# A slot's products with values stand between the two halves of the next slot's scores, in the normed and the causal attention of a decoder kernel

## The reference, cut to what matters

```
# L1 attention ("normed"): layernorm of q, k and v per head first
scores = jnp.einsum('bqhd,bkhd->bhqk', q, k) * scale
probs = jax.nn.softmax(scores, axis=-1)
out = jnp.einsum('bhqk,bkhd->bqhd', probs, v)
return out.reshape(b, s, NH * HD) @ Wo + bo

# L3 cross attention ("causal"): 77 context tokens stand ahead of x in keys and values
dots = jnp.einsum('bhid,bhjd->bhij', q, k) * scale
mask = j_idx > i_idx + mem_len
dots = jnp.where(mask[None, None], -jnp.inf, dots)
attn = jax.nn.softmax(dots, axis=-1)
```

## Time and profile before

| what | us |
|---|---|
| median of 3 runs | 9875.43 (9867.83 to 9891.36) |
| the profiled execution, its own time | 9900.52 |
| its span | 9898.7 |
| the normed stage's slots | about 2393 to 3492 |
| the causal stage's slots | about 7916 to 8768 |

### The profile page before, as it was taken

One profiled execution on the slowest core, in us unless ns is written; L12 is line 12 of the kernel. 1 busy time (PEld: TensorE's weight loads), 2 busy tenths in 40 slices (PEclk: granted clock), 3 DMA queues, 4 the chain that ended last, 5 costly groups with the idle time before them and its releaser, 6 DMA issues. The chain is left out here.

```text
span 9898.7 us, 124977 instructions
## 1 busy us (share of the span) xinstructions
PE 8326.5 (84%) x45542; PEld 4752.5 (48%) x45542; DVE 5787.9 (58%) x10909; ACT 4316.1 (44%) x7440; POOL 2034.5 (21%) x1786
## 2 busy tenths in 40 slices
PE   4888487985889979998998789888978699989998
PEld 1222255652333336645654344444434344458888
DVE  6778442025777736625643777874644365657776
ACT  3667231112555546514531556764312044444443
POOL 1110110211011001101100224432000011127776
PEclk8889666986999989999998889888977699989999
DMA  3222232212122100000000000000000133236665
GB/s 70 43 43 44 43 65 79 77 56 44 25 44 43 25 23 1 4 0 21 1 4 4 11 1 1 1 1 11 0 6 1 26 58 53 45 125 196 197 192 175
DMA packets 221123, 459.78 MB, mean 46 GB/s; under 512 B 51536, under 2 KB 87097, under 8 KB 219255
## 3 DMA queue, kind: packets, MB, share of 16 engines
q1 hardware_dynamic: 152935, 236.72, 11.9%
q0 software_dynamic: 67584, 215.02, 7.5%
HBM read 366.63 MB, written 71.33 MB: 44 GB/s over the span
## 5 line engine op out<-in xcount | busy, mean ns | idle before, releaser
L823 ACT ACTIVATE probs<-scores 128x1024 f32<-128x1024 f32 (+4 forms) x960 | 868.3, 937 | 885.0 <-PE scores L700 625.6
L912 DVE TENSOR_REDUCE row_max<-ring 128x1 f32<-128x512 f32 (+3 forms) x1792 | 1025.4, 626 | 239.3 <-PE ring L674 213.1
L700 PE MATMUL scores<-query_stack,key_stack 99*128 99x512 bf16 (+3 forms) x2816 | 853.9, 390 | 183.9 <-DVE levels L934 94.7
L3965 POOL DMA_INDIRECT r_got<-in_L_ffn_tables,r_index x768 | 784.7, 1022 | 453.9 <-DVE r_index L4261 202.5
L720 PE MATMUL outputs<-probs,head_values 128*32 128x512 f32 (+3 forms) x5632 | 764.9, 617 | 17.5 <-ACT probs L820 15.4
L820 ACT ACTIVATE probs<-levels,quant 128x1024 f32<-128x1024 uint8 x512 | 607.5, 1233 | 257.8 <-DVE levels L934 245.1
L674 PE MATMUL ring<-key_stack,query_stack 96*128 96x512 bf16 (+3 forms) x1792 | 608.7, 382 | 63.0 <-DMA key_stack<-normed_parts 39.6
L934 DVE TENSOR_SCALAR levels<-scores 128x1024 uint8<-128x1024 f32 x512 | 600.1, 1218 | 100.1 <-PE scores L700 96.7
L700 PEld LDWEIGHTS scores<-query_stack,key_stack 99*128 99x128 bf16 x2816 | 251.9, 103 | 714.9 <-DVE levels L934 310.1
L3783 DVE TENSOR_TENSOR_SCAN ssm_pre<-ssm_pre,added 128x1024 f32<-128x1024 f32 x256 | 571.0, 2271 | 31.2 <-ACT ssm_pre L3741 31.2
L3718 PE MATMUL state_sums<-term,constants 128*128 128x512 f32 x1024 | 497.9, 610 | 43.3 <-POOL term L3749 34.3
(11 more groups left out here) (695 smaller groups left out, 16237.8 us busy)
## 6 DMA issues: line engine op xcount, KB each, us to landing
joined_heads<-heads_out SPq DMA_DIRECT2D x512, 32.0 KB, 2.0
expert_w<-in_L_ffn_w SPq DMA_DIRECT2D x16, 1024.0 KB, 7.3
quant_parts<-parts SPq DMA_DIRECT2D x48, 256.0 KB, 5.5
query_stack<-quant_parts SPq DMA_DIRECT2D x48, 256.0 KB, 8.6
key_stack<-quant_parts SPq DMA_DIRECT2D x48, 256.0 KB, 8.4
query_stack<-cross_parts SPq DMA_DIRECT2D x48, 256.0 KB, 8.5
normed_parts<-parts SPq DMA_DIRECT2D x48, 256.0 KB, 5.2
query_stack<-normed_parts SPq DMA_DIRECT2D x48, 256.0 KB, 8.4
```

What stands on the lines that cost most here:

```text
L700: last = nc.tensor.matmul(out[:, off:GROUP], keys, q_stack[0:rows, h, half * GROUP + off:(half + 1) * GROUP], start=True, stop=not edge)
L823: nc.scalar.activation(dst, s_ps[0:k_rows, 2 * (e % 2):2 * (e % 2) + 2, off:GROUP], ACT.Exp, scale=scale).then_inc(probs_ready, 1)
L912: nc.vector.reduce_max(row_max[:, i, qt, at:at + 1], src[:, 0:cols], AX.X).then_inc(ring_read, 1)
L3965: nc.gpsimd.indirect_dma_start(out=got[:, k % GOT_ROWS, :], out_offset=None, in_=io["L3_ffn_tables"], in_offset=bass.IndirectOffsetOnAxis( ...
```

## The change

One line of `own_order` moves up by two: the products with values of slot n - 1 now stand behind place A of slot n and ahead of the second half of its scores.

```
             order += [("scores", n, 0)] if live else []
             order += [("values", n - 2)] if late and 0 <= n - 2 < len(slots) else []
             order += plan.get(3 * n, [])
+            order += [("values", n - 1)] if not late and 0 < n <= len(slots) else []
             order += [("scores", n, 1)] if live else []
             order += plan.get(3 * n + 1, [])
-            order += [("values", n - 1)] if not late and 0 < n <= len(slots) else []
             order += plan.get(3 * n + 2, [])
```

## The result

The changed kernel took 10041.86 us in the median of four runs (10035.65 to 10050.27), the kernel before 9875.85 (9867.83 to 9891.36, four runs): ratio 1.0167, 95% interval 1.0151 to 1.0183. That is +166 us where I had forecast +83, outside my range. The profiled execution took 10036.22 us (span 10034.1) against 9900.52 (span 9898.7), which is +136. The traces can only explain what is in them.

What follows compares the result with a forecast made beforehand. VectorE's reads through the three-bank ring bound mid-group slots, TensorE the projections, TensorE in step with ScalarE the tails. 48.3 + 4.7 + 9.1 + 21 = 83 us on 9875.4 gave 9958; 8-in-10 range 9905 to 10018.

Steps and rivals of the forecast that it cites:

- the ring's rule: Ring-bound slots, normed stage: gap W + 0.86 + 0.61 for each of the first n - 3 maxima; 48.3 us in sum.
- slot with sums: Ring-bound slots, normed stage: with five maxima TensorE's own work sets 3.88 us against 3.99, -0.1.
- the last group of the normed stage: Last sequence's group without maxima: 15 slots at 2.72 us instead of 2.115, costing 9.1 us.
- the step "tails", first half, the turn: The slot that ends in the turn, quiet groups of the normed stage: counted at +0.44 us like the other ring-bound slots.
- the step "tails", second half, the loop: Normed slots behind the maxima: values, second scores, exponent take 2.72 us a slot; +0.47 a tail, 4.7 us for ten.
- the step "causal stage": Whole causal stage: 21 us, estimated from three windows, with bounds of 8 and 45.
- the 4 us for tails and last group: Causal stage: 4 us for its tails and last group, less than normed because the diagonal slots have short values.
- slots of 6 to 9 us with float32 projections ... cost nothing: Slots with float32 projections: VectorE is half idle, TensorE's sum of work stays, so no cost.
- other slots of the busy groups: Groups with projections: 5.2 us each for normed third and first groups, 5.7 us for 8 causal groups.
- The clock: Rival, ring-bound slots: TensorE idles more often and its clock falls, adding 29 to 58 us, 9987 to 10016 us; 14%.
- The hiding ring: Rival, ring-bound slots: three banks hide the longer gap, the 48.3 us vanish, 18 remain, 9893 us; 8%.
- The earlier turn: Rival, group ends: VectorE sets the pace, last maxima up to 1.00 us earlier, 31 us back, 9862 us; 5%.

Runs made afterwards that it cites:

- narrow reads: VectorE reads 128 columns of each maximum instead of up to 512, in the changed kernel (10284.67 us, ratio 1.0033) and in the one before (10199.26 us, 0.9953).
- the kernel with the scores first: The changed kernel with its two blocks exchanged, the second half of the scores ahead of the values: +102 us against the kernel before.
- filled turn: Two float32 matmuls of constants ahead of each turn, in the changed order (10366.54 us, ratio 1.0109) and in the order before (10216.16 us, 0.9966).
- a step of any kind between the blocks: The changed kernel with the first step of B, whatever its kind, between the values and the second scores: +129 us against the kernel before.

## Why the prediction had the direction right and half the size

**Right: the ring's rule.** Gap + 0.86 + 0.61 for each further maximum gave 3.53 and 3.58 us, and 3.53 and 3.58 were measured; 3.05 with narrow reads shows the reads to be the cause, and the kernel with the scores first shows the gap to be. Without the slots that end in the turn, the middle of the quiet groups was forecast at 34.4 us in the normed stage and took 30.7. That the sum is so near is in part luck: one slot of each group took 0.91 us more where I had 0.44, and the first two slots, which I had left out, took 0.4 us less together. The other slot with sums took 4.18 us where I had 3.88, longer than before and not shorter. I let TensorE's own work bound it, which I had put at 2.98 us without sums and which is 3.05; why it takes 4.18 is not shown.

**Right: the last group of the normed stage.** 9.1 and 9.1 us: 2.78 us a slot, forecast 2.72, against 2.115 before, and the old order there takes it away to 0.1. That both are 9.1 to the tenth is chance: 15 slots at 2.78 would be 10.0.

**Failed: the step "tails", first half, the turn.** I gave the slot that ends in the turn 0.44 us. But the turn waits for the last read, and in the new order three maxima stand between the last values and the turn in place of two. So it is the scores and one read: 0.44 + 0.61 = 1.05, measured 1.03 (5.46 less 4.43), and the same at all eight quiet turns. The kernel with the scores first has the read alone, 5.03 less 4.43 = 0.60. In the causal stage one maximum became three: 0.44 + 2 x 0.61 = 1.66. There it is 8234.01 to 8237.93 before and 8320.56 to 8326.23 now, +1.75, where I had written 0.3:

```profile
8234.01 1.06 PE L720 MATMUL outputs<-probs,head_values 128*32 128x512 f32 x8
8235.00 0.39 PE L674 MATMUL ring<-key_stack,query_stack 96*128 96x512 bf16 x1
...
8237.93 0.23 PE L682 MATMUL ring<-identity_bf,top_parts 128*96 128x128 bf16 x1 [2.03 <-DVE top_parts L919]
```

```profile
8320.56 1.06 PE L720 MATMUL outputs<-probs,head_values 128*32 128x512 f32 x8
...
8322.12 0.38 PE L674 MATMUL ring<-key_stack,query_stack 96*128 96x512 bf16 x1
...
8322.39 0.60 PE L674 MATMUL ring<-key_stack,query_stack 96*128 96x512 bf16 x2
...
8326.23 0.31 PE L682 MATMUL ring<-identity_bf,top_parts 128*96 128x128 bf16 x1 [2.74 <-DVE top_parts L919]
```

**Failed: the step "tails", second half, the loop.** The loop's length was right (2.72 against 2.78) and so was the sum in a tail at full clock: three slots 8.33 us, forecast 8.16. With it the tail behind a filled turn is 0.66 us longer (8.52 less 7.86), where I had 0.47. What I missed stands around it: the 1.03 us at the turn, where I had 0.44, and the clock. I took the 7.16 us of the earlier trace rows for the tail of before, and that is one of the few at 1.00; at most turns of both kernels it falls, and the forecast has no term for it. The normed tails of quiet groups took 26.3 us, 3.3 each, where 3.5 + 4.7 = 8.2 was forecast for the turns of quiet groups and all tails; the order accounts for 1.69 of the 3.3 at the filled turn. The rest is not split between the clock and the waits for the loaded rows. In the busy groups these waits did hide the cost, as forecast: their normed turns came 1.63 or 2.64 us later, the scores' wait for the rows fell from 38.0 to 0.9 us in the stage, and the tails took 7.7 us less.

**Failed: the step "causal stage".** 21 us became 62.6, outside my bounds of 8 to 45. The largest piece is the 4 us for tails and last group, "less than in the normed stage because the diagonal slots have short values". They took 19.8 - 1.5 + 9.5 = 27.8 us. Short values do not help enough: 9.5 us of this is the last group alone, and the turn's extra reads, 1.75 us at each quiet turn, are paid in this stage most. The slots that I worked out by the rule were the smaller miss, 19.7 against 11.4.

**Failed: "slots of 6 to 9 us with float32 projections ... cost nothing".** VectorE is half idle there, but not in the half that counts. The forecast's 10.4 + 5.7 us, all of it for other slots of the busy groups, became 27.9 + 15.1. In the one slot that I followed (L760, L956) a maximum behind such a step needs a bank which VectorE has still to read, and the values had been covering that. For the causal stage the gap between the ring's steps is the cause, as a step of any kind between the blocks takes most of it away (15.1 to 5.5); for the normed stage the cause is open.

**The rivals.** The clock fell, but not where the rival said: the ring-bound slots kept 1.00, it fell behind the turns, and there it had fallen in the kernel before too. Its part in the difference was some 16 us by the pair of filled kernels, and not told from nothing. By the Trainium skill, "TensorE: Matmul & The Clock Gate", section "A second HAM failure mode: psum-queue depth-cycling", short idling between groups of matmuls on PSUM banks makes the clock swing, in a kernel measured there. The ring-bound slots do not bear that out here: TensorE's waits of 0.2 us ahead of the maxima in the slots of 3.53 us left the clock at 1.00. Waits of 2.0 to 3.2 us ahead of the turn were followed by a lower clock at 51 of the 60 turns of the two kernels. The hiding ring fell with 3.53 us; its sum has a slip, since it names a third of the causal estimate and adds 4 us, where a third of 21 is 7. The earlier turn fell too: the turn came 1.03 us later.

What stays open: the 30 us between the profiled pair's difference and that of the medians, the normed busy groups' 28 us, and what of the tails is clock.

## What to carry to other kernels

When a block of TensorE's queue moves, write down for every place not only how long the stretch without a step for the consumer becomes, but also what the block had been covering where it stood: here a read of VectorE that the next matmul's bank waits for. Work out the places where the steady rhythm ends (the turn, the tail, the group without maxima) with the same care as the rhythm: they had most of the error. Look at all places of one kind before taking one of them for the price: the tail in the earlier trace rows was one of five at full clock out of thirty. A wait of 2 to 3 us on TensorE that can't be removed can be worth filling with matmuls that nobody reads, where a dense stretch follows it: here it was, in both orders.

## What the runs showed of the hardware that I had not expected

In both kernels TensorE waits 2.0 to 3.2 us ahead of each turn, and in the 8 us behind it the granted clock was below 1.00 at 51 of 60 turns. At the changed kernel's turn shown it was 2.78 us of waiting, after 2.69 us of work in 5.46, then 0.82, and four scores took 1.77 us instead of 1.04. The same wait does not always do it: in the kernel before 2.39 us were followed by 1.00 in the earlier trace rows and by 0.79 at another turn of the stage, where the values take 1.94 us and not 1.06:

```profile
2527.67 0.23 PE L682 MATMUL ring<-identity_bf,top_parts 128*96 128x128 bf16 x1 [2.39 <-DVE top_parts L919]
2528.66 1.94 PE L720 MATMUL outputs<-probs,head_values 128*32 128x512 f32 x8
```

```profile
2527.70:2535.70 8.00, 7.88 (x38) 1.57 (x39) 0.28 (x1) 4.90 (x5) 0.00 (x0) 0.79 0.03 8
```

With the wait filled the clock was 1.00 at 53 of 60 turns and at no turn under 0.91. Filling it cost TensorE 30 matmuls in each stage (60 in the counting of the profile) and gave the kernel before 35 to 41 us of 10257. I had not looked for that in its own profile, though it was there.
